# Rotary projection: the rotated rows move into a PSUM bank, and three banks instead of four take turns

## The reference, cut to what matters

```python
h = _rms(x, w_ln1)                                   # x was layer-normed before
q = (h @ wq + bq).reshape(B, S, N_HEADS, HEAD_DIM)   # 16 heads of 32
k = (h @ wk + bk).reshape(B, S, N_KV, HEAD_DIM)
v = (h @ wv + bv).reshape(B, S, N_KV, HEAD_DIM)
q, k = q * cos + rot(q) * sin, k * cos + rot(k) * sin   # rot: halves swapped, one negated
```

## Time and profile before

| | us |
|---|---|
| median of 3 runs | 2204.81 (2203.09 to 2207.2) |
| the profiled execution, its own time | 2203.34 |
| its span in the profile | 2201.6 |
| the rotary projection in it: first matmul of unit 0 to last rotation (L733) | 1033.34 to 1185.35 |

### The profile page before, as it was taken

The page is one execution under the profiler, slowest core; times in us unless marked ns, Lnnn a source line. Parts: engine busy times, 40 slices in busy tenths (PEclk is TensorE's granted clock), DMA queues, the critical chain, the costliest instruction groups (busy, mean ns, idle before and its releaser), DMA issues.

```text
span 2201.6 us, 31494 instructions
## 1 busy us (share of the span) xinstructions
PE 2027.0 (92%) x10679; PEld 1360.0 (62%) x10679; DVE 1210.9 (55%) x2649; ACT 906.3 (41%) x1699; POOL 694.9 (32%) x610
## 2 busy tenths in 40 slices
PE   7999999788699999996998999978999999999998
PEld 6876666566333333334776666657888887555554
DVE  6446666376689898875876666535323153121221
ACT  3435554355377676773443545434212221111111
POOL 0004655246323132322564755601000000233332
PEclk9997999999799999998997999989999999999999
DMA  5637766357654545444566766462111045233332
GB/s 196 221 155 161 167 159 134 112 191 264 210 138 119 148 110 148 100 126 120 191 211 202 167 152 154 112 219 96 43 54 60 18 179 222 56 65 62 62 61 37
DMA packets 150706, 297.15 MB, mean 135 GB/s; under 512 B 24530, under 2 KB 43092, under 8 KB 149524
## 3 DMA queue, kind: packets, MB, share of 16 engines
q1 hardware_dynamic: 112676, 241.64, 37.4%
q10 hardware_dynamic: 29136, 34.87, 6.0%
q0 software_dynamic: 8736, 18.62, 4.5%
HBM read 181.55 MB, written 102.50 MB: 129 GB/s over the span
## 4 chain that ended last, share of the span: by engine, by line
PE 43%; DVE 4%; DMA 3%; ACT 1%; issue 1%; POOL 1%; SPq 1%; ACTq 0%; POOLq 0%; DVEq 0%
PE bank L1702 10%; PE bank L1790 8%; PE bank L1713 5%; PE bank L1809 4%; PE bank L461 3%; PE bank L1083 2%; PE bank L1114 2%; PE bank L1155 2%; PE bank L1172 2%; DMA stack<-rotary_c_max_rows 1%; DMA normed<-xt 1%; PE bank L1123 1%; PE bank L1774 1%; PE bank L1117 1%; DVE rotary_p_hn L695 1%
## 5 line engine op out<-in xcount | busy, mean ns | idle before, releaser
L1275 ACT ACTIVATE cross_c_prob<-bank 128x512 f32<-128x512 f32 x512 | 271.0, 598 | 117.0 <-PE bank L1114 115.9
L1316 DVE TENSOR_REDUCE row_max<-bank 128x2 f32<-128x1024 f32 x256 | 299.7, 1212 | 27.4 <-PE bank L1083 26.4
L1702 PE MATMUL bank<-moe_hT,moe_w 128*128 128x512 f32 x1056 | 251.5, 394 | 10.1 <-DVE moe_prod L2075 5.5
L1083 PE MATMUL bank<-stack 48*128 48x512 f32 (+4 forms) x768 | 209.9, 454 | 39.8 <-PEq L71 24.4
L1114 PE MATMUL bank<-stack 56*128 56x512 f32 (+4 forms) x768 | 233.7, 429 | 13.1 <-DMA stack<-rotary_c_max_rows 5.3
L1702 PEld LDWEIGHTS bank<-moe_hT,moe_w 128*128 128x128 f32 x1056 | 199.8, 190 | 53.3 <-DVE moe_prod L2075 5.9
L1114 PEld LDWEIGHTS bank<-stack 56*128 56x128 f32 (+1 forms) x768 | 118.7, 193 | 144.1 <-ACT cross_c_prob L1275 68.9
L1790 PE MATMUL bank<-moe_w_e,moe_hT_e 128*128 x624 | 194.4, 465 | 4.4 <-DMA moe_w_e<-in_experts_packed 3.9
L1083 PEld LDWEIGHTS bank<-stack 48*128 48x128 f32 (+1 forms) x768 | 103.8, 201 | 121.0 <-DVE row_max L1316 50.3
L1790 PEld LDWEIGHTS bank<-moe_w_e,moe_hT_e 128*128 128x128 f32 x624 | 116.3, 191 | 66.1 <-issue 8.5
L1312 DVE CUSTOM_DVE_ANT_0 first_c_masked<-bank,later 128x128 f32<-128x128 f32 (+3 forms) x256 | 115.4, 485 | 71.2 <-PE bank L1083 70.3
(11 more groups left out here) (361 smaller groups left out, 4009.2 us busy)
## 6 DMA issues: line engine op xcount, KB each, us to landing
moe_w_e<-in_experts_packed SPq DMA_DIRECT2D x8, 2176.0 KB, 8.6
qk_parts<-first_p_parts SPq DMA_DIRECT2D x32, 512.0 KB, 2.8
stack<-qk_parts SPq DMA_DIRECT2D x64, 256.0 KB, 6.5
qk_parts<-cross_p_parts SPq DMA_DIRECT2D x32, 512.0 KB, 2.7
stack<-qk_parts SPq DMA_DIRECT2D x256, 64.0 KB, 2.5
qk_parts<-rotary_p_parts SPq DMA_DIRECT2D x32, 512.0 KB, 2.7
moe_raw<-in_shared_packed SPq DMA_DIRECT2D x11, 768.0 KB, 10.7
stack<-qk_parts SPq DMA_DIRECT2D x16, 512.0 KB, 5.2
```

The source lines that it names most:

```text
L1083: last = nc.tensor.matmul(bank[:, 0 : width_q(m)], q_stack[slot][r : r + PRODUCT_ROWS, at, m * P : (m + 1) * P], k_stack[slot][r : r + PRO ...
L1275: nc.scalar.activation(probability(g, step // HEADS_AT_ONCE, step % HEADS_AT_ONCE), psum[bank_at["score", n]][:, 0 : S - q0], ACT.Exp).the ...
L1316: nc.vector.tensor_reduce(row_max[:, g % 2, m, j - 1 : j + 1], c.banks[:, first : first + WIDE, :], AX_X, ALU.max).then_inc(s.max_done, 1)
L1702: last = nc.tensor.matmul(psum[bank][:], weights(pa, f, k), hT[p % 2][:, pb, k, :], start=m == 0, stop=m == len(steps) - 1)
```

## The change

Three edits, all in `projection_phase`, and all of effect in the rotary layer alone (`rope` is true for `cross` and `rotary`, and `cross` did all three before):

- the ring has banks 5, 6, 7 instead of 4, 5, 6, 7, and the sum is written to bank 4 instead of over `turned`;
- DVE's sum of unit i waits until `low` of unit i-1 is done (bank 4 holds one unit at a time);
- POOL's cosine product of unit i waits for the sum of unit i-1 instead of `low` of unit i-2.

```diff
-        ring_banks = (5, 6, 7) if cross else (4, 5, 6, 7)
-        rotated_at = lambda i: psum[4] if cross else turned[:, i % 2]
+        ring_banks = (5, 6, 7) if rope else (4, 5, 6, 7)
+        rotated_at = lambda i: psum[4]
...
-                        if cross and i:
+                        if i:
                             dve.wait_ge(s.parts_lo, i)
                         nc.vector.tensor_tensor(rotated_at(i), turned[:, i % 2], swapped[:, i % 2], ALU.add).then_inc(s.rotated, 1)
...
-                            if cross and i:
+                            if i:
                                 pool.wait_ge(s.rotated, i)
-                            elif i >= 2:
-                                pool.wait_ge(s.parts_lo, i - 1)
                             nc.gpsimd.tensor_tensor(turned[:, i % 2], straight[:, i % 2], cos_t[:, i // n_qk if cross else 0], ALU.mult).then_inc(s.cos_made, 1)
```

## The result

The changed kernel took 2213.85 us, median of 7 runs (2207.34 to 2217.93), beside 2204.81 for the kernel before in as many; the ratio is 1.0037, 95% interval 1.0021 to 1.0053. So it is slower, by 8.2 us as the ratio has it (4.6 to 11.7), where 7.1 had been forecast; the medians lie 9.0 apart, and 2213.85 is some 2 above the 2211.9 forecast beside the median. The profiled execution has a span of 2213.0 us, 11.4 more than before, and part of that lies outside the stage that was changed: unit 0 of the rotary projection started at 1035.99 instead of 1033.34 although everything ahead of it is the same code. Over the eleven profiled executions of this study that start lies from 1032.6 to 1037.9 us in ten and at 1042.8 in one.

What follows compares the result with a forecast made beforehand. PE bounds the rotary projection whenever it may run; 1.2 + 5.5 - 0.3 + 0.8 - 0.1 = 7.1 us on 2203.34 gave 2210.4, or 2211.9 beside the runs' median. Range for 8 in 10: 2206 to 2216.5.

Steps and rivals of the forecast that it cites:

- The bank that goes: Rotary ring: unit n waits for unit n-3, costing net 1.2 us in batch 0 and 5.5 at two gates.
- two gates: Releases of v1 in batches 1 and 2, fixed to their batch's start by the `h1` store; 2.73 us lost at each.
- The 0.3 given back: Transposes behind the gates: 0.3 us subtracted from the forecast sum.
- The wait in front of the sum: DVE's sum waits for `low` of the unit before: 0.2 us each, 0.4 a gate, 0.8 in all.
- the relief: `low` reading a bank no longer collides with POOL: real but mostly off the path, so no gain counted.
- The clock: PE's slow stretches at the two gates: nothing counted, open end of 1.1 us either way.
- the first rival: Clock also falls behind batch 0's new wait, costing 1.7 to 2.8 us: about 2215.5; chance 0.14.
- POOL and two SBUF inputs: POOL and DVE instructions with two SBUF inputs exclude each other: first square 1.79 us instead of about 0.6.
- The second rival: DVE's squares keep POOL out: four take 2.45 us instead of 4.65, total +1.0, 2205.8 us; chance 0.09.
- The forecast's own sign: DVE's squares in the new trace: the first two still around 1.8 us.
- The bank as source: Rotary `low` reading from a bank: 0.66 to 0.70 us throughout.
- The tail: After the last q and k, POOL and sum form a ring: rounds 3.44 instead of 3.48, 0.1 us back.

Runs made afterwards that it cites:

- the ring alone: Kernel before with the rotary ring on banks 5, 6, 7, bank 4 unused, sum in SBUF and waits as before: 2215.65 us, ratio 1.0044.
- waits_only: Kernel before with both edited waits (DVE's sum, POOL's cosine product), four banks, sum in SBUF: 2208.38 us, ratio 1.0024.

## Why the prediction was right

- **The bank that goes.** Forecast 1.2 in batch 0 and 2.7 at each of two gates, less 0.3. Unit 12 starts 27.93 us behind unit 3, 26.67 before: 1.26. From unit 12 to unit 24 is 41.94 and was 38.96: 2.98, of which 0.28 is a later gate (27.56 from unit 12 to the release, 27.28 before) and 2.7 the unit behind it. From unit 24 to unit 36 is 43.47 and was 40.60: 2.87, of which 0.43 is a later gate. These three make 7.1. With the ring alone they came out as 1.06, 2.65 and 2.67, 6.4 together. The mechanism is the forecast one: the release hardly moves and a whole unit comes to lie behind it.
- **The 0.3 given back.** No run shows this term, and that the sum came out with it is luck. The transposes of batch 2 do run at full clock now, but a slow stretch costs about half its length whether matmuls or transposes fall into it (a matmul started every 0.43 us at 0.50, and the 16 transposes at 1025.98 took 3.67 us at that level, where at full clock a matmul starts every 0.227 us and batch 1's 16 transposes took 1.75), so moving the transposes out of it gives nothing back by itself. With the ring alone they ran at full clock too, the stretch reached into q3 instead, and from unit 24 to 36 the whole unit was paid, 2.67 us with the gate no later. In the changed kernel's trace that stretch happened to end some 0.5 us sooner behind the gate, which is the 0.3. The stretch that follows the held unit, in before, after and the ring alone (length, busy times, granted clock):

```profile
1141.80:1142.70 0.90, 0.90 (x7) 0.90 (x6) 0.90 (x1) 0.66 (x1) 0.90 (x2) 0.63 1.01 405
```
```profile
1149.80:1150.70 0.90, 0.90 (x5) 0.77 (x4) 0.83 (x2) 0.00 (x0) 0.60 (x1) 0.94 0.99 394
```
```profile
1149.80:1150.70 0.90, 0.90 (x4) 0.74 (x3) 0.90 (x1) 0.00 (x0) 0.90 (x2) 0.59 0.99 398
```

- **The wait in front of the sum.** Forecast 0.4 a gate. By the after trace it is 0.28 at the first and 0.43 at the second. The difference between the ring alone and the whole change is 0.7 for everything beside the ring, where the forecast had 0.8 at the gates and 0.2 in batch 0, less 0.1; the cheaper slow stretches hide some 0.4 more. The size held, but the reasoning was too simple. The waits alone cost 5.0 us with the sum in SBUF. They are cheap in the change because the bank takes `low` out of POOL's way (1.8 us), and because the late PE hides DVE's rest, which is argued from the waits that are gone in front of units 12, 24 and 36. I had booked the relief as off the path; in the tail it is on it, since without the bank the new waits lengthen the tail by 1.7 us. That the terms add up to 7.1 to the tenth, with the clock moving by some tenths from run to run, is luck.
- **The clock.** Forecast nothing lost or gained, with 1.1 either way as an open end. The first unit behind the gates took 4.44 and 5.29 us, 4.45 and 5.29 before. The two places that were set against the first rival in the cross layer, behind 1.76 and 1.44 us of idle, have a granted clock of 1.00 (from 467.5 to 469.5 and from 510.8 to 512.0). In the windows below (stretch, its length, busy times, granted clock) the second gate shows the low level throughout, the first one shows it up to about 1105.4 (0.50 from 1102.3) and nearly full clock behind that (0.93 from 1105.4 to 1106.4), and the 1.38 us of idle in front of unit 8 left the clock at its full level (1.00), so the first rival is out:

```profile
1101.90:1106.40 4.50, 4.46 (x13) 3.52 (x14) 3.31 (x7) 2.63 (x6) 2.32 (x2) 0.62 1.04 299
1144.50:1149.80 5.30, 5.30 (x13) 4.16 (x14) 3.81 (x8) 3.20 (x6) 2.53 (x2) 0.50 0.60 195
...
1061.60:1067.00 5.40, 5.40 (x24) 4.47 (x25) 3.89 (x8) 3.21 (x6) 2.56 (x2) 1.00 0.42 166
```

- **POOL and two SBUF inputs.** That POOL and a DVE instruction with two SBUF inputs keep each other out is read from these durations. The rotary projection before (least, median and greatest duration in ns; the square is `h1` times `h1`, both inputs in SBUF):

```profile
L695 DVE CUSTOM_DVE_ANT_0 rotary_p_hn<-rotary_p_h x12: 679/1217/1795, 1052.5 to 1135.0; 128x512 f32<-128x512 f32 x12
L830 POOL TENSOR_TENSOR rotary_p_turned<-rotary_p_straight,rotary_p_cos_t x32: 1273/1608/1622, 1038.8 to 1181.3; 128x512 f32<-128x512 f32 x32
L832 POOL TENSOR_TENSOR rotary_p_swapped<-rotary_p_swapped,rotary_p_sin_t x32: 1282/1296/1763, 1040.4 to 1182.8; 128x512 f32<-128x512 f32 x32
```

Six of the 12 squares overlap with a product of POOL (by over 0.1 us) and take 1.75 to 1.79 us, the other six 0.68. Ten of the 32 `low`s do and take 0.93 to 1.82, the other 22 at most 0.69: the one at 1061.02 began 0.01 us behind a product of POOL that took 1.29, and took 1.82. After, `low` reads a bank: 13 overlap with a product and take 0.66 to 0.69. A v read-out, with one input in a bank, takes 0.67 to 0.69 beside POOL (11 before, 12 after) and the shuffle, with one input, 0.72 to 0.77 (17 and 18). Of POOL's 64 products after, the six that overlap with a square take 1.58 to 1.74 us, the other 58 take 1.26 to 1.31, 42 of them beside some other instruction of DVE. So the numbers in the forecast's sentence stand but for two: a square by itself takes 0.68 us, and 0.6 is the distance of two starts (0.61); and the product beside the first square was the cosine one with 1.61, the 1.74 lay beside the second.
- **The second rival** had the order right for one square and wrong for the row; the row of squares is 0.1 us shorter, not 2.2. The forecast's own sign, the first two squares at 1.8, failed for the first (0.68). POOL got its turn after one square and again after the next: 0.68, 1.75, 1.74 and 0.68 us.
- **The bank as source.** It makes no `low` longer: `low` from the bank has a median of 675 ns, and from SBUF 680 over all 32 before, ten of them beside POOL; the least are 659 and 661.
- **The tail.** Forecast 0.1 back; unit 47 to the last sum is 5.36 us and was 5.38. That the new waits and the undisturbed products cancel held: with the waits and the sum in SBUF it is 7.1.
- **Outside the stage.** The ratio's 8.2 us and the stage's 7.1 agree within the interval (4.6 to 11.7 us). The rest of the 11.4 between the two profiled executions lies ahead of unit 3 (3.3) and behind the last sum (1.0), in unchanged code; that it is scatter is supported by the spread of unit 0's start over the runs, not shown for this pair.

## What to carry to other kernels

One bank less in this ring cost a unit of work, 2.7 us, at each of two releases that did not depend on PE's progress, and 1.1 to 1.4 at a release that came just too late: find the latest release, see which unit it holds and what PE could still have done ahead of it. Look at the release's own anchor before the banks: here it stood in SP's queue behind stores that come late, and moving one store gave 9.7 us in L, more than any arrangement of the banks cost. Costs measured alone need not add up: ring 6.4, waits 5.0, and with the bank as the sum's place 7.1 together. And a stage with slow stretches of the clock in it does not repeat to the tenth: here those stretches alone moved by 1.2 us.

## What the runs showed of the hardware that I had not expected

In `waits_only` DVE's `low` beside POOL's sine product, both 128x512 with two inputs in SBUF, cost POOL 0.44 us a round even when `low` itself only took 1.20 instead of 0.68: POOL's product went from 1.29 to 1.73 us, and a dependent round from 3.48 to 3.91.

The wait of DVE for its own `low`, just ahead of the sum, made the step from one to the other about 0.2 us longer (0.81 from `low` to sum in the changed kernel, 0.59 before). Alone that is small; in the run with this wait alone unit 12 started 0.9 us later.

The length of PE's idle time did not order what followed it: behind 4.49 and 4.53 us the first unit took 4.44 and 5.29 us, behind 2.54 and 3.07 us it took 4.45 and 5.29, behind 3.67 with the waits alone 4.44. With v1 read out first, two stops of nearly the same length differed: behind 2.21 us the clock fell, to 0.69 in the mean, behind 2.20 it did not (1.00; the 4 us behind the transposes in either case, the granted clock third from the end):

```profile
1113.20:1117.20 4.00, 4.00 (x15) 3.21 (x14) 3.19 (x7) 2.91 (x5) 3.07 (x3) 0.69 0.96 350
1153.40:1157.40 4.00, 4.00 (x21) 3.31 (x19) 3.05 (x7) 3.87 (x8) 2.99 (x3) 1.00 0.61 241
```
